# Flamingo block, second attention and its neighbours: order of steps changed on three engines

## What is computed

```
def layernorm(x):
    return (x - mean(x)) / sqrt(var(x) + 1e-5)

def linear8(x, w, b):                      # w8a8
    sx = max(max|x| over channels / 127, 1e-8);  qx = clip(round(x / sx), -127, 127)
    sw = the same over each row of w;            qw = likewise
    return (qx @ qw.T) * (sx * sw) + b
...
# attention of layer 3: 16 heads of 16 channels, 64 queries and 64 keys a sequence
q = linear8(layernorm(x), wq, bq);  k = ctx @ wk'.T + bk;  v = ctx @ wv'.T + bv
o = softmax(q k' / 4 + mask) v
x = x + tanh(g) * linear8(o, wo, bo)
# feed-forward of layer 3: rounded tokens and rounded weights
h = silu(bit_linear(xn, gate_w, gate_b)) * bit_linear(xn, val_w, val_b)
x = x + tanh(g) * bit_linear(h, out_w, out_b)
```

## Time and profile before

| | us |
|---|---|
| median of three runs | 1678.53 |
| the three runs | 1678.53, 1668.43, 1678.97 |
| the profiled execution, its time | 1667.83 |
| its span, first to last instruction | 1666.0 |

### The profile page before, as it was taken

One profiled execution on the slowest core, in us unless ns is written; L12 is line 12 of the kernel. 1 busy time (PEld: TensorE's weight loads), 2 busy tenths in 40 slices (PEclk: granted clock), 3 DMA queues, 4 the chain that ended last, 5 costly groups with the idle time before them and its releaser, 6 DMA issues.

```text
span 1666.0 us, 20163 instructions
## 1 busy us (share of the span) xinstructions
PE 1282.5 (77%) x6670; PEld 724.6 (43%) x6670; DVE 1022.4 (61%) x2512; ACT 475.9 (29%) x664; POOL 327.7 (20%) x319
## 2 busy tenths in 40 slices
PE   0128999999889899777777344545898889899997
PEld 0104454544434466444554222222454445455554
DVE  8994454444262466657876788883788778832222
ACT  3462222222122233222222122220454445441110
POOL 2120000000025200042234232224343324100000
PEclk9987999999999999988888566665999989999999
DMA  9000000011000100001110000002222223100001
GB/s 314 25 13 1 0 0 0 0 59 45 20 1 0 64 1 0 19 7 26 25 25 0 20 1 0 0 1 78 85 87 78 78 72 91 49 1 0 0 0 50
DMA packets 67472, 55.72 MB, mean 33 GB/s; under 512 B 23888, under 2 KB 60624, under 8 KB 67152
## 3 DMA queue, kind: packets, MB, share of 16 engines
q1 hardware_dynamic: 66768, 54.67, 10.9%
q10 hardware_dynamic: 640, 0.26, 0.1%
HBM read 39.97 MB, written 14.68 MB: 33 GB/s over the span
## 4 chain that ended last, share of the span: by engine, by line
PE 60%; issue 17%; DVE 13%; POOL 5%; ACT 2%; DMA 1%; DVEq 0%; SPq 0%; POOLq 0%; ACTq 0%
PE banks L1022 7%; PE banks L2012 7%; PE banks L421 6%; PE banks L638 5%; PE banks L417 5%; PE banks L855 3%; PE banks L1029 3%; POOL sb_work L1447 3%; PE banks L847 3%; PE banks L428 3%; PE banks L432 2%; PE banks L1977 2%; PE banks L1640 1%; DVE sb_work L2250 1%; PE banks L1962 1%
## 5 line engine op out<-in xcount | busy, mean ns | idle before, releaser
L2250 DVE TENSOR_REDUCE sb_work<-banks 128x2 f32<-128x512 f32 x256 | 164.7, 685 | 51.6 <-PE banks L1977 49.3
L2121 ACT ACTIVATE sb_work<-banks 128x1024 f32<-128x1024 f32 x128 | 130.9, 1023 | 135.3 <-PE banks L1998 135.2
L538 DVE TENSOR_TENSOR sb_work<-sb_work,banks 128x512 f32<-128x512 f32 x72 | 49.4, 686 | 125.3 <-ACT sb_work L505 125.3
L1447 POOL TENSOR_TENSOR sb_work<-sb_work,sb_consts 128x512 f32<-128x512 f32 x64 | 66.7, 1072 | 268.6 <-ACT sb_work L1395 230.8
L1022 PE MATMUL banks<-sb_work,sb_shelf 128*128 128x512 f32 x256 | 114.4, 592 | 0.0
L421 PE MATMUL banks<-sb_work,sb_shelf 128*128 128x512 f32 (+1 forms) x192 | 93.9, 640 | 8.6 <-DVE sb_work L581 8.6
L638 PE MATMUL banks<-sb_work,sb_ctx_nat 128*64 128x512 f32 (+15 forms) x512 | 89.9, 510 | 7.8 <-DVE sb_work L700 7.8
L505 ACT ACTIVATE sb_work<-banks 128x512 f32<-128x512 f32 x72 | 42.9, 596 | 183.3 <-PE banks L417 116.2
L998 POOL TENSOR_TENSOR sb_late<-sb_w2n 128x1024 f32<-128x1024 f32 x10 | 22.7, 2268 | 363.9 <-DVE sb_work L692 363.3
L1101 DVE TENSOR_TENSOR sb_work<-sb_work,banks 128x512 f32<-128x512 f32 x32 | 22.0, 687 | 110.6 <-ACT sb_work L1087 110.6
L417 PE MATMUL banks<-sb_work,sb_shelf 128*128 128x512 f32 (+1 forms) x192 | 84.9, 593 | 0.0
(11 more groups left out here) (287 smaller groups left out, 2525.6 us busy)
## 6 DMA issues: line engine op xcount, KB each, us to landing
sb_work<-scratch SPq DMA_DIRECT2D x64, 192.0 KB
scratch<-sb_work SPq DMA_DIRECT2D x32, 192.0 KB, 2.1
sb_work<-ctx_t SPq DMA_DIRECT2D x16, 256.0 KB, 4.2
scratch<-sb_work SPq DMA_DIRECT2D x32, 128.0 KB, 2.1
sb_work<-ctx_t SPq DMA_DIRECT2D x4, 512.0 KB, 3.7
sb_ctx_nat<-ctx SPq DMA_DIRECT2D x1, 2048.0 KB, 11.0
sb_raw<-wguT SPq DMA_DIRECT2D x1, 2048.0 KB, 15.2
scratch<-sb_work SPq DMA_DIRECT2D x32, 64.0 KB, 1.8
```

The lines of the kernel that those rows point to most:

```text
L1447: ins = nc.gpsimd.tensor_tensor(km_[:, hf, k, :, :], keys.unsqueeze(1).broadcast_to([P, 8, SEQ]), hm2.unsqueeze(2).broadcast_to([P, 8, SEQ ...
L2121: nc.scalar.activation(pt3[:, h % 2, :, :], o, ACT.Exp).then_inc(exp3, 1)
L2250: nc.vector.tensor_reduce(out=mx3[:, tc, k, 2 * hp:2 * hp + 2], in_=bank[u % 2].rearrange("p (h s) -> p h s", h=2), axis=AX, op=ALU.max).t ...
```

## The change

Four edits. (1) In attn2 the turn of the weights is a function of its own, `turn_weights`, and PE's loop becomes scores(t+1), turn_weights(t), values(t+1), weigh(t); on DVE the scores are handled ahead of the tile's values (`shifted_scores`, `own_values`). (2) At the end of a block the next block's queries are served first on all engines: DVE rounds them behind tile 2 and scales them ahead of the output, PE turns and multiplies them ahead of o's product; o is turned through bank 6 in place of bank 0. The norm's three steps go one behind each of tiles 0, 1 and 2. (3) In bit both halves of tile t + 1 are issued ahead of `out_proj(t - 1)`. (4) A Newton round has three instructions in place of four, in all calls of the root.

```
-                link(nc.vector.tensor_tensor(t, y, y, ALU.mult))
+                link(nc.vector.scalar_tensor_tensor(out=t, in0=y, scalar=-0.5, in1=y, op0=ALU.mult, op1=ALU.mult))
                 link(nc.vector.tensor_tensor(t, t, v, ALU.mult))
-                link(nc.vector.tensor_scalar(t, t, -0.5, 1.5, ALU.mult, ALU.add))
-                link(nc.vector.tensor_tensor(y, y, t, ALU.mult))
+                link(nc.vector.scalar_tensor_tensor(out=y, in0=t, scalar=1.5, in1=y, op0=ALU.add, op1=ALU.mult))
...
# attn2, PE
                 for t in range(BT):
                     if t + 1 < BT:
                         scores(b, t + 1)
+                    turn_weights(b, t)
+                    if t + 1 < BT:
                         values(b, t + 1)
-                    attend(b, t)
+                    weigh(b, t)
                 if not last:
                     keys(b + 1)
+                    query_ints(b + 1)
                 pe.wait_ge(o_int_ready, b + 1)
-                turn_ints(o_int, 0).then_inc(o_int_turned, 1)
+                turn_ints(o_int, 6).then_inc(o_int_turned, 1)
+                if not last:
+                    queries(b + 1)
                 pe.wait_ge(o_intT_ready, b + 1)
                 by_weights(o_intT, woT2, 1).then_inc(out2_done, 1)
                 if not last:
-                    query_ints(b + 1)
-                    queries(b + 1)
+                    turn_queries(b + 1)
...
# attn2, DVE (first() is split: own_values() has its first half, shifted_scores() the rest)
-                first(b, 0)
+                shifted_scores(b, 0)
+                own_values(b, 0)
                 for t in range(BT):
                     if t + 1 < BT:
-                        first(b, t + 1)
+                        shifted_scores(b, t + 1)
+                        own_values(b, t + 1)
                     second(b, t)
-                    if t == 2:
-                        normalise(link, (b + 1) % BLOCKS)
+                    if t < 3:
+                        normalise(link, (b + 1) % BLOCKS, step=t)
+                    if t == 2 and not last:
+                        query_ints(b + 1)
                 dve.wait_ge(o2_ready, BT * b + BT)
                 quantise(link, o_mid, o_mid, o_int, 1.0 / 127.0, 1e-8).then_inc(o_int_ready, 1)
                 if not last:
-                    query_ints(b + 1)
+                    queries(b + 1)
                 dve.wait_ge(out2_done, b + 1)
                 link(scaled(o_mid, 1, qs, so_b))
...
                 nc.vector.tensor_tensor(xs, xs, o_mid, ALU.add).then_inc(x_done, 1)
-                if not last:
-                    queries(b + 1)
...
# attn2, ACT
                 if not last:
                     keys(b + 1)
-                ints(b, o_int_turned, o_intT, 0, o_intT_ready)
+                    query_ints(b + 1)
+                ints(b, o_int_turned, o_intT, 6, o_intT_ready)
...
# bit, PE
                 gate_value(b, 1, 0)
+                gate_value(b, 1, 1)
                 for t in range(1, BT):
-                    gate_value(b, t, 1)
                     if t + 1 < BT:
-                        gate_value(b, t + 1, 0)
+                        for f in range(2):
+                            gate_value(b, t + 1, f)
                     out_proj(b, t - 1)
```

More of the change, by code:

```diff
@@ L131, in rsqrt @@
             for _ in range(3):
-                link(nc.vector.tensor_tensor(t, y, y, ALU.mult))
+                link(nc.vector.scalar_tensor_tensor(out=t, in0=y, scalar=-0.5, in1=y, op0=ALU.mult, op1=ALU.mult))
                 link(nc.vector.tensor_tensor(t, t, v, ALU.mult))
-                link(nc.vector.tensor_scalar(t, t, -0.5, 1.5, ALU.mult, ALU.add))
-                link(nc.vector.tensor_tensor(y, y, t, ALU.mult))
-        LN_LINKS = 18
+                link(nc.vector.scalar_tensor_tensor(out=y, in0=t, scalar=1.5, in1=y, op0=ALU.add, op1=ALU.mult))
+        LN_LINKS = 15
         def statistics(link, b):
@@ L955, in ternary_vector @@
             with dve.Fori(0, BLOCKS - 1) as b:
-                link.enter(b, 16 + LN_LINKS)
+                link.enter(b, 13 + LN_LINKS)
                 block_(b, False)
@@ L1320, in scores, with turn_weights @@
                     ins.then_inc(scored, 1)
-            def attend(b, t):
+            def turn_weights(b, t):
                 pe.wait_ge(exp2, BT * b + t + 1)
@@ L1329, in attend, with weigh @@
                 ins.then_inc(pt2_turned, 1)
+            def weigh(b, t):
                 pe.wait_ge(pt2_ready, BT * b + t + 1)
@@ L1356, in queries, with turn_queries @@
                 by_weights(q_intT, wqT2, 4).then_inc(q2_done, 1)
+            def turn_queries(b):
                 pe.wait_ge(q2_ready, b + 1)
@@ L1386, in attn2_tensor @@
             queries(0)
+            turn_queries(0)
             with pe.Fori(0, BLOCKS - 1) as b:
@@ L1400, in ints, with query_ints @@
                 nc.scalar.activation(dst.rearrange("p c n -> p (c n)"), bf_bank(i), ACT.Copy).then_inc(ready, 1)
+            def query_ints(b):
+                ints(b, q_int_turned, q_intT, 3, q_intT_ready)
             def queries(b):
-                ints(b, q_int_turned, q_intT, 3, q_intT_ready)
                 act.wait_ge(q2_turned, b + 1)
@@ L1431, in attn2_scalar @@
             keys(0)
+            query_ints(0)
             queries(0)
@@ L1458, in attn2_vector, with shifted_scores @@
             dve.wait_ge(masks_in, 16)
-            def first(b, t):
-                dve.wait_ge(v2_done, BT * b + t + 1)
-                if t >= 2:
-                    dve.wait_ge(pv2_done, BT * b + t - 1)
-                def heads(v, par):
-                    return v.rearrange("p (h w d) -> p h w d", w=2, d=D2)[:, :, par, :]
-                for k in range(2):
-                    for par in range(2):
-                        ins = nc.vector.scalar_tensor_tensor(
-                            out=vm[:, t % 2, k, :, par * D2:(par + 1) * D2],
-                            in0=heads(bank[7][:, k * DIM:(k + 1) * DIM], par),
-                            scalar=half_of[par], in1=heads(bv_b, par), op0=ALU.mult, op1=ALU.add)
-                ins.then_inc(v2_ready, 1)
+            def shifted_scores(b, t):
                 if t >= 2:
@@ L1488, in first, with own_values, heads @@
                                         ALU.subtract).then_inc(sc_shift, 1)
+            def own_values(b, t):
+                dve.wait_ge(v2_done, BT * b + t + 1)
+                if t >= 2:
+                    dve.wait_ge(pv2_done, BT * b + t - 1)
+                def heads(v, par):
+                    return v.rearrange("p (h w d) -> p h w d", w=2, d=D2)[:, :, par, :]
+                for k in range(2):
+                    for par in range(2):
+                        ins = nc.vector.scalar_tensor_tensor(
+                            out=vm[:, t % 2, k, :, par * D2:(par + 1) * D2],
+                            in0=heads(bank[7][:, k * DIM:(k + 1) * DIM], par),
+                            scalar=half_of[par], in1=heads(bv_b, par), op0=ALU.mult, op1=ALU.add)
+                ins.then_inc(v2_ready, 1)
             def second(b, t):
```

## The result

The changed kernel took **1609.97 us** (median of 4, 1608.79 to 1614.21) beside 1673.48 of the kernel before (median of 4, 1664.70 to 1678.97). The ratio is 0.963, with a 95% interval of 0.9576 to 0.9683. 1641.6 was forecast. The profiled spans are 1666.0 and 1608.1, 57.9 apart, where the sum had 31.8, so the change gained 1.8 times what the sum held. TensorE's mean granted clock went from 0.891 to 0.914.

The account below looks back on a forecast made before the run. DVE was taken to bound bit, a chain between engines attn2. Attn2 7.0 (with port stall), bit 15.2 and the root 9.6 make 31.8 us; off 1673.4, the middle of four runs, that gives 1641.6, range 1623 to 1661.

Parts of the forecast that it names:

- The port stall of the statistics: In attn2, the moved statistics on DVE wait for POOL's masked keys: 0 to 1.9 us a block, taken as 1.9.
- The loop of attn2: Turn and values exchanged, norm moved into the loop: with the stall, the last exponential ends 1.2 us later a block.
- The last chunk in bit: DVE's wait before the last chunk of each block goes, less 0.4 given back beside POOL: 4 x 3.8 = 15.2 us.
- The root in wkv: Five norms in wkv, 0.6 us less a call: 3.0 us.
- (a): Rival: no port stall for such small steps in attn2; 39.4 us gained, 1634; chance 0.25.
- (c): Rival: bit's gap stays because POOL's product or ACT's silu comes last; 15.2 us less gained, 1657; chance 0.08.
- (d): Rival: TensorE stays at the lower clock level through attn2's whole loops; 60 us lost, 1702; chance 0.05.
- Rival (b): TensorE's clock falls one tile earlier in attn2: 5 us more in 4 blocks, 20 lost, 1661; chance 0.12.
- part 4: The root: three fewer links are 0.6 us a call, counted in wkv, ternary, bit and attn3; 9.6 us together.
- The tail of attn2: End of a block: scaling the next queries ahead of the output takes 3.16 us off the chain to the scores, taken as 3.0.
- the collision of the earlier trace: Third block of attn2: the queries' scalings met POOL (4.37 us for 1.6); moved behind tile 2 they don't: 2.8 us.
- Part 1: attn2's loop, turn and values exchanged: 3 x 1.2 us gained on PE a block, spent again but for 0.7 without stall.

Follow-up runs that it names:

- e1: The kernel before with edit 4 alone (three instructions a Newton round); 1639.45 us, ratio 0.9841.
- e5: e1 with 75 memsets added on DVE in moe, so attn3's loop stands where it stood in the kernel before; 1653.07 us, ratio 0.9893.
- e6: The kernel before with 53 memsets added on DVE in moe, moving attn3's loop in DVE's list; 1659.12 us, ratio 0.994.
- e14: The changed kernel with 73 memsets, so attn3's loop starts where it did in the kernel before; 1621.27 us, ratio 0.9687.
- e4: The kernel before, unchanged, profiled a second time; one execution, 1664.61 us.
- e13: The kernel before with 128 memsets on DVE in moe, moving attn3's loop 128 instructions further on; 1667.13 us, ratio 0.9998.
- e2: The kernel before with edits 1 and 2 alone (attn2); 1653.84 us, ratio 0.9922.
- e8: The kernel before with edit 1 alone (turn and values exchanged in attn2); 1659.6 us, ratio 0.9935.
- e10: e8 with POOL waiting at attn2's block ends, but the last, until DVE has rounded o and the next queries; 1648.08 us, ratio 0.9894.
- e3: The kernel before with edit 3 alone (bit); 1650.42 us, ratio 0.9885.
- e11: e9 with TensorE's queries' product ahead of o's turn at attn2's block end; 1596.08 us, ratio 0.9573.
- e9: The changed kernel with the whole norm behind tile 2 in attn2 and POOL held until o is rounded; 1600.17 us, ratio 0.961.
- e12: e11 with the norm's statistics ahead of a block's first scores; 1617.32 us, ratio 0.9716.

## Why the prediction was wrong

**Right by its steps.** The port stall of the statistics: 1.9 us more was taken, 2.4 measured. The loop of attn2 against before, from first to last exponential: 1.2 us a block lost was forecast, 1.4 to 2.7 measured (22.0 us before; 23.7, 23.4, 24.6 and 24.2 after). The last chunk in bit: 3.8 a block; its read came 5.6, 5.6, 5.2 and 5.6 us behind the one before it and comes 1.3 behind now, 3.9 to 4.3 less (the sum's "4 x 4.20" had one wait of 3.79 in it). The root in wkv: 3.0. TensorE's clock in attn2 is 0.85 beside 0.84 in the earlier trace rows. Rivals (a), (c) and (d) didn't happen.

**Rival (b) happened in part, without its cost.** In three of the four blocks TensorE's clock did fall to half behind the wait for the exponential of tile 2, as in the second:

```profile
791.56 1.59 PE L1326 MATMUL banks<-sb_ident,sb_work 128*128 128x128 f32 x8 [2.17 <-ACT sb_work L1421]
792.95 3.12 PE L1304 MATMUL banks<-sb_shelf,sb_work 128*128 128x256 f32 x8
```

At full clock they take 1.09 and 1.89. TensorE only waited less for the exponential of tile 3 (1.49 us here, 3.16 in the first block), so the loop took no more time (23.4 us and 23.7). The rival's 5 us a block took TensorE for the path where DVE was.

**The port stall was read from the wrong kind of row.** Both meetings in the earlier trace rows are of steps with one input in SBUF (L1123, L1128), not two, so they didn't bear out the rule of two inputs that the prediction cites. That such steps of 0.16 us stall beside POOL is first shown by the changed kernel (L145, L147, and L148, which has one input).

**The step that failed most: part 4.** "Three fewer are 0.6 a call", nothing else, made 9.6 us; e1 measured 26.5. Of this, 7 to 8 are the hole in attn3 (e5, e6, e14). The sum priced the root by its instructions' time and not by their number in DVE's list; in a loop each of them counts twice there, for `link` adds a register step. That this took the loop to a place where it fits is luck: 53 instructions more did it, too (e6). In the third block of attn2 e1 won 2.9 us, since the rounding that met POOL in the earlier trace rows no longer did, but its first block was 1.8 longer, and attn2 gave 1.3 in all. In the changed kernel attn3 gave 15.3 us. 7.9 are the hole and what follows it, by e14. Some 3.2 belong to the profiled execution of the kernel before: e4 and e13, with the same attn3 and the hole, are 3.3 and 3.1 shorter there. 4.2 are left, of which the root was to give 1.8.

**The tail of attn2 was mis-sized.** 3.0 us were forecast for a block's end; from its last exponential to the next block's first, 5.7 and 5.6 were measured at the first two. The scaling of the queries moved up by 3.8, not 3.2. Then the values of the next block ran at full clock (1.89 us at 816.33, 3.42 before), 1.5 more. The third was forecast with 5.8 and gave 9.1: the same 5.7, and 3.4 for the collision of the earlier trace rows, forecast with 2.8. Ends of 5.7, 5.6 and 9.1 less loops of 8.0 make 12.4, and with the stage's beginning 13.1, not 7.0. The blocks are 50.4, 49.9 and 51.1 us apart, not 52.3. Edit 2 was not run by itself: e2 (both) less e8 (the exchange) leaves 2.5 us of attn2 for it.

**Part 1's reading that the norm "hid beside PE's tile 3"** is half of it. What the exchange wins in the loop (e8, 3.4 us a block) the block's end gives back, as long as norm and roundings stand there and POOL runs into them; with POOL held back (e10) it gives back 0.5 and 1.0 us at the first two.

**The clock.** Stages in which no edit was active moved in lumps of 1.7 us: ternary lost 1.7 in e2 and e3, and with the changed kernel's ternary it gained 6.1 in that kernel and e11, but 4.4 in e9, e12 and e14. The same eight products of bit, in the kernel before, then in e3:

```profile
1039.96 3.59 PE L1640 MATMUL banks<-sb_late,sb_work 128*128 128x512 bf16 x8 [1.19 <-ACT sb_work L1697]
```

```profile
1036.17 1.90 PE L1640 MATMUL banks<-sb_late,sb_work 128*128 128x512 bf16 x8 [1.19 <-ACT sb_work L1698]
```

3.59 us is half clock, 1.90 full; the idle time ahead is the same 1.19. Two such lumps in ternary (3.4) and one in bit (1.7) would be most of what these stages gave beyond the forecast (3.7 and 2.4); that is a reading, no run set it. Why it fell there and not here I haven't settled; it was seen, not set.

**The level.** 1673.4 was taken as a middle between two levels. In the 47 executions of the kernel before since, the medians are 1667.3 to 1669.3, and four are above 1675 (the highest is 1682.3): the forecast started some 5 us too high. The other 26 of the 31.6 us by which it missed are in the steps above.

## What to carry to other kernels

Where two engines share a port, look at the end of a block for pairs that only just miss each other, and ask which of the two moves when a step ahead gets faster; a wait on the engine with time to spare (e9, e10) was worth 6.6 to 10.2 us in this stage. Count a change in instructions, too: on an engine whose loop hardly fits, taking out three of them a call, or adding 53 elsewhere, moved the time by 7 to 8 us. Its sign is an idle time that ends with "issue" at a loop's branch back, together with more pieces on the instruction queue. Time each edit alone before believing a sum: here the smallest edit had the largest gain.

## What the runs showed of the hardware

- DVE's instructions come in pieces of 128 (8 KB, by the queue's rows: 31 pieces, 0.25 MB). A loop of 300 to 306 instructions that touched four pieces had five brought in its second round and cost 4.6 to 5.6 us of idle DVE at the branch back to its head; one that touched three had none and no idle time beyond 0.2 to 0.3 us.
- The stall beside POOL isn't only for instructions with two inputs in SBUF: a step with one (L148, 0.97 for 0.16; the roundings, 3.23 for 1.14, and 1.42 for 0.69) waits too. Scalings that read a PSUM bank and one SBUF row (1.66 at 813.68) and reductions (1.22) beside POOL's products took their usual time. The Trainium skill, page "SBUF — State Buffer", section "Who interferes with whom", has this: tensor_scalar can take the shared pair, tensor_reduce can't. The traces agree. The forecast used only its rule for two inputs.
- A DVE step of 0.16 us that meets POOL costs the rest of one POOL instruction: about 1.0 us beside a 128x512 product, 2.27 beside the 128x1024 bias.
